# Attention and a low-rank feed-forward block on one core: the low part of the rotated queries made by GpSimd in place of VectorE

## What is computed

```python
q = rmsnorm(h @ Wq_a) @ Wq_b                    # rank 192; 32 heads of 128 + 64 (the 64 are rotated)
ckv = h @ Wkv_a                                 # 64 compressed + 64 rotated key columns, shared by all heads
k_nope, v = split(rmsnorm(ckv[..., :64]) @ Wkv_b)
probs = softmax(causal((qf @ kf.T) * scale))
x = x + layernorm((probs @ v).reshape(b, s, H * VD) @ Wo)     # h = layernorm(x)
x = x + layernorm(ffn(layernorm(x)))            # tiled weights with low-rank additions, silu gate
```

## Time and profile before

| | us |
|---|---|
| median of 3 runs | 649.94 (647.52 to 650.62) |
| the profiled execution | 649.47 |
| its span | 647.7 |
| PE busy | 604.4 (93%) |
| DVE busy | 524.9 (81%) |
| ACT busy | 412.9 (64%) |
| POOL busy | 166.4 (26%) |

### The profile page before, as it was taken

How to read it: one execution, slowest core, us unless ns; L and a number is a source line. 1 busy time by engine, 2 the same in 40 slices (tenths; PEclk the granted TensorE clock), 3 DMA queues, 4 the chain that set the end, 5 groups by cost and what they waited for, 6 DMA issues and landing times.

```text
span 647.7 us, 12397 instructions
## 1 busy us (share of the span) xinstructions
PE 604.4 (93%) x3432; PEld 446.3 (69%) x3432; DVE 524.9 (81%) x1292; ACT 412.9 (64%) x1157; POOL 166.4 (26%) x137
## 2 busy tenths in 40 slices
PE   5778999999999999999999999999999988879996
PEld 4566667767777777677677766775777766656664
DVE  5987788888888888888888898889868888867456
ACT  4455777868777777777777777788732343155343
POOL 2011322122213212221232122212034433125520
PEclk9998999999999999999999999999999999969999
DMA  8000211201202102112022021112670000001003
GB/s 323 15 1 1 82 45 38 81 22 58 81 0 81 58 23 81 36 45 81 0 81 81 0 81 39 42 53 98 206 289 1 0 1 1 29 1 50 0 17 114
DMA packets 13862, 37.80 MB, mean 58 GB/s; under 512 B 1328, under 2 KB 1584, under 8 KB 13584
## 3 DMA queue, kind: packets, MB, share of 16 engines
q1 hardware_dynamic: 13840, 37.53, 17.2%
HBM read 31.24 MB, written 6.29 MB: 58 GB/s over the span
## 4 chain that ended last, share of the span: by engine, by line
PE 71%; DVE 17%; ACT 4%; issue 3%; DMA 3%; SPq 0%; DVEq 0%; ACTq 0%
PE bank L1003 13%; PE bank L1015 12%; PE bank L962 11%; PE bank L964 11%; PE bank L963 11%; DVE dot L833 4%; PE bank L1033 2%; PE bank L1025 2%; PE bank L972 2%; PE bank L986 2%; PE bank L985 2%; DMA x<-x 2%; PE bank L1182 2%; DVE st L809 2%; DVE xn L817 1%
## 5 line engine op out<-in xcount | busy, mean ns | idle before, releaser
L367 ACT ACTIVATE pr<-ss,small 128x128 f32<-128x128 f32 (+3 forms) x256 | 143.1, 559 | 41.4 <-DVE small L635 40.8
L375 ACT ACTIVATE pt<-bank 128x128 f32<-128x128 f32 (+3 forms) x256 | 110.8, 433 | 60.5 <-PE bank L1003 60.4
L635 DVE CUSTOM_DVE_ANT_0 ss<-bank,cst 128x128 f32<-128x128 f32 (+3 forms) x256 | 123.2, 486 | 13.3 <-PE bank L964 8.8
L1003 PE MATMUL bank<-ident,pr 128*128 128x128 f32 x640 | 118.9, 284 | 3.2 <-ACT pr L367 3.0
L1003 PEld LDWEIGHTS bank<-ident,pr 128*128 128x128 f32 x640 | 75.6, 142 | 66.8 <-ACT pr L367 34.1
L284 POOL TENSOR_TENSOR qrot<-qrot,qswp 64x512 f32<-64x512 f32 x64 | 82.6, 1290 | 137.4 <-DVE qrot L621 137.4
L962 PE MATMUL bank<-kt_hi,qt_hi 128*128 128x128 f32 (+3 forms) x256 | 100.9, 394 | 3.6 <-DVE qt_lo L625 2.7
L1015 PE MATMUL bank<-pt,kvn 128*64 128x256 f32 (+3 forms) x512 | 86.2, 448 | 0.7 <-ACT pt L375 0.7
L964 PE MATMUL bank<-kt_hi,qt_lo 128*128 128x128 f32 (+3 forms) x256 | 83.2, 325 | 0.0
L963 PE MATMUL bank<-kt_lo,qt_hi 128*128 128x128 f32 (+3 forms) x256 | 83.0, 324 | 0.0
L625 DVE TENSOR_TENSOR qt_lo<-qrot,qt_hi 128x512 fp32r<-128x512 f32 x64 | 60.2, 941 | 24.6 <-ACT qt_hi L357 24.5
(11 more groups left out here) (168 smaller groups left out, 1171.4 us busy)
## 6 DMA issues: line engine op xcount, KB each, us to landing
sv<-sv SPq DMA_DIRECT2D x16, 576.0 KB, 3.7
sq<-sq SPq DMA_DIRECT2D x16, 448.0 KB, 3.4
wvo_scratch<-vs SPq DMA_DIRECT2D x16, 256.0 KB, 2.1
wv_raw<-wvo_scratch SPq DMA_DIRECT2D x8, 512.0 KB, 4.1
xa<-x SPq DMA_DIRECT2D x8, 256.0 KB, 5.3
x<-x SPq DMA_DIRECT2D x1, 2048.0 KB, 11.0
out<-yo SPq DMA_DIRECT2D x8, 256.0 KB, 2.0
w<-w SPq DMA_DIRECT2D x1, 1376.0 KB, 13.6
```

Source lines behind the costliest of these rows:

```text
L367: nc.scalar.activation(pr[:, k % 4, 0:n], ss[:, k % 2, 0:n], ACT.Exp, bias=negmax[:, k % 8:k % 8 + 1], scale=-1.0, accum_out=rsum[:, k:k + ...
L375: nc.scalar.activation(pt[:, b, h, 0:i + 1, i * P:(i + 1) * P], bank[2 + k % 2][:, 0:(i + 1) * P].rearrange("p (j q) -> p j q", q=P), ACT. ...
L635: nc.vector.tensor_tensor_reduce(out=ss[:, k % 2, 0:n], in0=bank[k % 2][:, 0:n], in1=mask[:, SEQ - n:SEQ], scale=-SCALE, scalar=3.4e38, op ...
L1003: last = nc.tensor.transpose(bank[2 + k % 2][:, j * P:(j + 1) * P], pr[:, k % 4, j * P:(j + 1) * P], ident[:, :])
```

## The change

`query_lo` leaves VectorE's program and enters GpSimd's. On VectorE nothing takes its place. On GpSimd both low parts of a batch stand behind both rotation sums of that batch; only the first two queries of all alternate (sum, low part, sum, low part), with a wait for the low part before the next sum. The waits of the moved instruction are the old one (for `qt_hi`) and one for the sums, which GpSimd itself makes. The consumers are unchanged.

```diff
--- before.py
+++ after.py
@@ -284,6 +284,13 @@
                 nc.gpsimd.tensor_tensor(qrot[RKV:P, h, :], qrot[RKV:P, h, :], qswp[RKV:P, h, :], ALU.add)\
                   .then_inc(a.pe_added, 1)
 
+            def query_lo(gi, b, h, added):
+
+                pool.wait_ge(a.pe_added, added)
+                pool.wait_ge(a.qt_hi_made, gi + 1)
+                nc.gpsimd.tensor_tensor(qt_lo[:, b, h, :], qrot[:, h, :], qt_hi[:, b, h, :].bitcast(F32), ALU.subtract)\
+                  .then_inc(a.qt_split, 1)
+
             def spread(m, added, first=False):
 
                 pool.wait_ge(a.pe_added, added)
@@ -298,14 +305,22 @@
             def body(p, first=False, last=False):
                 for h in range(2):
                     add_rotated(4 * p + 2 + h, h, 2 * p if h == 0 and not first else None)
+                for h in range(2):
+                    query_lo(4 * p + 2 + h, 1, h, 4 * p + 4)
                 spread(2 * p, 4 * p + 4, first)
                 if not last:
                     for h in range(2):
                         add_rotated(4 * p + 4 + h, h, 2 * p + 1 if h == 0 else None)
+                    for h in range(2):
+                        query_lo(4 * p + 4 + h, 0, h, 4 * p + 6)
                 spread(2 * p + 1, 4 * p + (4 if last else 6))
 
-            for h in range(2):
-                add_rotated(h, h)
+            add_rotated(0, 0)
+            query_lo(0, 0, 0, 1)
+            pool.wait_ge(a.qt_split, 1)
+            add_rotated(1, 1)
+            query_lo(1, 0, 1, 2)
+            pool.wait_ge(a.qt_split, 2)
             body(0, first=True)
             with nc.gpsimd.Fori(1, PAIRS - 1) as p:
                 body(p)
@@ -620,11 +635,6 @@
                     dve.wait_ge(a.qt_split, gi - 1)
                 nc.vector.tensor_tensor(qrot[:, h, :], bank[6 + h][:, :], cos1, ALU.mult).then_inc(a.q_rotated, 1)
 
-            def query_lo(gi, b, h):
-                dve.wait_ge(a.qt_hi_made, gi + 1)
-                nc.vector.tensor_tensor(qt_lo[:, b, h, :], qrot[:, h, :], qt_hi[:, b, h, :].bitcast(F32), ALU.subtract)\
-                  .then_inc(a.qt_split, 1)
-
             def mask_and_max(U, k, first=False):
 
                 n = P * (k % QB + 1)
@@ -701,8 +711,6 @@
                             rotate_swapped(gi + 1, 1)
                         elif r in (0, 2) and not (first and k == 0):
                             rotate_own(gi + r // 2, r // 2)
-                        if r in (3, 5):
-                            query_lo(gi + r // 2 - 1, b, r // 2 - 1)
                         if r == 7 and not last:
                             rotate_swapped(gi + 2, 0)
                     if k == 6 and not first:
@@ -781,9 +789,6 @@
                 if t in (TB, TB + 1):
                     rotate_swapped(t - TB, t - TB, first=True)
                     rotate_own(t - TB, t - TB, first=True)
-                if t in (TB + 1, TB + 3):
-                    h = (t - TB - 1) // 2
-                    query_lo(h, 0, h)
                 if t in (TB + 2, TB + 3):
                     mask_and_max(t - TB - 2, t - TB - 2, first=True)
 
```

## The result

| | before | after |
|---|---|---|
| median, 20 runs each | 649.29 us | 651.59 us |
| the profiled execution | 649.47 | 652.17 |
| its span | 647.7 | 650.3 |
| DVE busy | 524.9 | 475.2 (73%), 1228 instructions |
| POOL busy | 166.4 | 247.3 (38%), 201 instructions |

Two of the 20 runs after the change (835.6 and 1708.2 us) were slow ones and are left out of the ratio; without them the median would be 651.55.

A forecast was written before the change was run, and what follows sets the result against it. TensorE was taken to set the pace (25.49 of 25.66 us a loop pair). Terms 0.65 + 2.2 + 0.8 - 0.35 = +3.3 us on 649.47 gave 652.8, plus 0.47 for the median: 653.2; range 650.2 to 656.8.

The forecast's parts named there:

- the side: Whole kernel: slower by 3.3 us, on the 0.5% (3.25 us) bound; chances slower 0.48, same 0.47, faster 0.05.
- Start, +0.65: Start of attention: GpSimd's first low part delays VectorE's `kvn` job and TensorE's transpose; +0.65 us, bounds 0 and +1.2.
- the start costs little: Rival, 21%: VectorE's `sq` jobs pass in time, one meeting at most; start terms 0.4 + 0.8, total +1.6, 651.6 us.
- First pair, +2.2: First pair: VectorE's two `sq` jobs wait behind GpSimd's low parts, so TensorE's query product starts later; +2.2 us.
- a rival: Rival, 22%: longer idle stretches lower TensorE's clock (+1 at most) and GpSimd's own wait is longer; +5.6, 655.5 us.
- Loop, +0.06 a pair: Loop: scores 0.39 late (own wait 0.19, to weight load 0.05), old 0.33 stall before transposes gone; +0.8 over 14 pairs.
- Last pair, -0.35: Last pair: TensorE's 0.59 wait for an exponential behind both `qt_lo` shortens; -0.35 us, between 0 and -0.6.
- faster: Rival, 7%: loop low part ready before 292.40, whole stall won (14 x 0.33 = 4.6); with small start terms -3.8, 646.1 us.

The follow-up runs named there:

- pair0_on_vector: The change, but VectorE keeps the low parts of queries 2 and 3, which ran beside its split of the new query weights; 649.12 us, ratio 0.9996.
- loop_only: The change, but only from query 4 on: the low parts of queries 0 to 3 stay on VectorE; 649.49 us, ratio 1.0001.
- first_half_only: The change only in first halves of the loop's pairs (sum, low part, sum, low part) and the last pair (old order); rest on VectorE; 643.15 us, ratio 0.9906.
- pair0_low_waits: The change, but in the first pair GpSimd's two low parts wait until VectorE has split the new query weights; 648.50 us, ratio 0.9988.
- low_before_sum: The change, but in first halves of pairs after the first, GpSimd makes the first query's low part before the second query's sum; 647.44 us, ratio 0.9972.
- low_later: The change, but in each loop pair's first half GpSimd first repeats columns 0 to 255, delaying the first low part; 663.55 us, ratio 1.0225.

## Why the prediction was right, step by step

651.6 lies inside 650.2 to 656.8 and 1.6 below the forecast of 653.2. The ratio is 1.0035: the side was right, the bound of 0.5% was not passed.

- **Start, +0.65: wrong, it is 0.** It rested on GpSimd holding the `kvn` job for 1.1 us. The two started 0.03 apart and the `kvn` job was not held (0.21). The transpose came 0.34 earlier. `pair0_on_vector`, which has the start on GpSimd, is 0.4 below `loop_only`, which has not: nothing, within their intervals. The rival "the start costs little" had half of the truth, this half.
- **First pair, +2.2: right in mechanism and place.** Both `sq` jobs passed a whole low part each, as the order 58.06 against 58.19 said, and the product came 2.27 later. 0.43 of that had come from earlier (GpSimd's sum stood at 57.02 for 56.59). That part belongs to the clock's phase: with the code of before up to there, the sum stands at 57.71 in `loop_only` and at 58.04 in `first_half_only`. So the meeting is 1.84 where 2.2 was forecast; about 1 us of clock comes on top, which I had only in a rival. Together 2.8 by the landmarks, 2.5 to 3.1 by the medians (`pair0_on_vector`, `pair0_low_waits`).
- **Loop, +0.06 a pair: right, but two of its parts were off.** GpSimd's own wait was 0.09, not 0.19, and from its end (296.37 to 296.39) to the scores were 0.13 instead of 0.05. The scores are 0.37 late (0.39 forecast), the old stall of 0.33 went, a pair is longer by 0.38/14 = 0.03. `low_before_sum` and `low_later` show that the stalls were worth about their full length: 0.39 a pair gained on the change and 0.36 on the kernel before, 0.81 a pair lost for a delay of 0.82.
- **Last pair, -0.35: right**, -0.42 by the landmarks.
- **The sum.** With the measured terms: 0 + 2.8 + 0.4 - 0.4 = 2.8; the medians differ by 2.3, the forecast was 3.3. Some of the nearness is luck: the 0.65 of the start that did not come and the 0.6 that the first pair had too little cancel. Of the 1.6 us between 653.2 and 651.59 another 0.65 is the base, 649.94 from three runs where twenty give 649.29. The rival "the start costs little" gave 651.6, the measured time, but through `sq` jobs that pass in time, which they did not. And the lower end of the range took 0.4 + 1.1 for the start terms whose own lower bounds were 0. In the profiled executions 3.49 us are lost at the last `sv` product (447.63 and 451.12) and 2.6 at the end; the rest comes back behind attention, where the code is the same, because TensorE's clock rose earlier there:

```profile
576.00:578.00 2.00, 2.00 (x6) 1.59 (x5) 2.00 (x3) 0.46 (x1) 0.37 (x1) 0.52 0.00 0
```

```profile
579.50:581.50 2.00, 2.00 (x10) 1.63 (x9) 2.00 (x3) 1.18 (x4) 0.37 (x1) 1.00 0.00 0
```

(Before, from 576 to 578; after, 579.5 to 581.5, which is the same work, 3.5 us later.) Over twelve kernels with the same code behind attention this does not go with the meeting: from the last `sv` product to the last table load of ScalarE it is 176.9 to 177.9 us with it and 176.8 to 178.5 without. I take it for the phase of the clock and not for the change.

**What I had not seen** is that the change, which costs 2.3 us, makes a gain of 6 us possible. The rival "faster" was weighed only by whether the low part would be ready in the order that the change wrote. It needed one step more: GpSimd stands idle for 3.89 us before the second sum, the high part is made in that gap, and most of the low part fits there.

## What to carry to other kernels

When work moves from VectorE to GpSimd, look first at what VectorE does in the same microseconds: here its jobs with two SBUF inputs of 0.29 us took 1.09 and 1.26 beside GpSimd instructions of 1.28, and TensorE's clock stayed low for longer behind the idle stretch that came of it. A wait that keeps the two apart, or cutting the GpSimd job, removed the whole cost here. Then place the moved job in its new engine's idle time, not behind the work that is due there: the same instruction made a pair 0.03 us longer in one place of the order and 0.36 shorter in another, and in the last pair, where its neighbours came at other times, the first place was the better one.

## What the hardware showed that I had not expected

- A GpSimd job that waits for its own engine's result starts 0.09 us behind the sum (293.73 + 1.28 to 295.10), 0.16 where an explicit wait stood between low part and sum (288.44 + 1.28 to 289.88). Two low parts in a row take 2.53, 1.26 each.
- The add over 64 partitions and the subtraction over 128 take the same, 1276 and 1293 ns on average: the time goes by columns. 256 columns take 0.74, 128 about 0.43.
- Of a GpSimd and a VectorE job 0.02 to 0.04 us apart, the one that started second was not held, and the first got 0.10 longer (all eight kernels with the start on GpSimd show it: 1.37 to 1.39 us against 1.28).
- A stage whose code no run changed varies: from the last `sv` product to the last table load 176.8 to 178.5 us in the profiled executions, which I put down to the clock's phase. Differences under a microsecond between two kernels' medians can be this alone; the lengths between landmarks inside the loop repeat better (359.59 to 359.63 in five kernels with the change's loop; 353.73 to 354.20 in four with the new order).
